# Second attention: the sum of the added columns and the inverse sums at the head of VectorE's step

## The chip, the cores and the metric

The kernel runs on one core of a Trainium2 chip. The metric is the device time of one execution in microseconds (us). A core has five engines with a queue each, which run their instructions in order and meet through semaphores: TensorE (PE, with its weight loads as PEld), VectorE (DVE), ScalarE (ACT), GpSimd (POOL) and SyncE (SP), which issues DMAs.

## The reference

Two blocks of a gated network run over x of 16 batches x 256 rows x 512 columns, each a cross attention and a feed-forward. The part that matters here is the second attention, `_L1_xattn_ref`, with 16 heads of 32 columns:

```python
y_dca, y_main = y[:, -16:, :], y[:, :-16, :]           # 16 added rows, 240 own rows
k_dca = _ln(kv_dca[:, :, 0], kn_dca_w, kn_dca_b);  v_dca = kv_dca[:, :, 1]
q = _ln((x @ Wq + bq).reshape(b, s1, H, HD), qn_w, qn_b)
k = _ln(kv[..., :HD], kn_w, kn_b);  v = kv[..., HD:]
ctx = _attn(q, k, v) + _attn(q, k_dca, v_dca)           # two softmaxes, one sum
return ctx @ Wo + bo
```

Each query row thus has two softmaxes per head, one over 240 columns and one over 16 added ones, each with its own sum.

## The kernel before

The change is in `gated_normed_attention`, the third of four stages of the program (2150 to 2866 us of the span). It runs over 16 batches; a batch has 16 heads in 4 groups of 4, taken in pairs: 8 pairs a batch (`PAIRS`), 128 in all. Every engine has a function `step(i, u)`, called for u from -13 up: `u` is the pair's number (two batches make a turn `i` of the loop), and the order in each queue is the order of the statements in that function. What a batch needs besides its pairs (projections, norms, the output) is placed on steps by a table (`plan`, `due`), with the next batch's work on the steps of the present one. Modulo 8, on VectorE: k0 is taken in step 7 and k1 late in it, q0 in step 1 (late), q1 in 2, v1 in 3, v0 in 4, o0 in 5, o1 in 6; head sums (`head_sums`) are in steps 1 and 3, the statistics in 7, eleven links of an inverse square root (`links`, `root_step`, lines 1903 to 1911) in 3, 4 and 5. A taking reads a projection out of one of two PSUM banks (`room`), adds a bias and frees the bank; TensorE's next product in that bank waits for it (`wait_room`). Batches 2 to 5 (`MADE`) have their k and v loaded from memory: there TensorE has no k and v units, and VectorE's takings of them read SBUF.

A pair n goes this way. TensorE makes the scores (line 2066). VectorE, in step n-1, takes the negated maxima (2530, 2531) and adds that of the 16 added columns (2533). ScalarE, in step n, takes the exponential of the added columns (2180, `d_done`) and of the own ones in four pieces, whose sums it accumulates (2182, an activation and an accumulator read each; `e_done` after the last). In even steps the last two pieces stand behind the copies `copy_pt` and `ot_hi`, which wait for TensorE. VectorE, in step n+1, sums the added columns' exponentials (2491, `d_summed`) and takes the inverse of both sums (2504, `r_done`), which waits for `e_done` and `d_summed`. GpSimd multiplies the probabilities with it (2275 the added columns, 2277 twice the own ones, `p_done`), and then has in some steps the scaling of a group of q and k (2290), a sum with the output's bias (2300) and the gathers (2260). TensorE, in step n+2, turns both heads (2077) through one bank, `ptb`, which ScalarE copies out each time (2192, `pt_done`), and multiplies with v (2091) once a group is whole. Scaled groups of q and k are turned at line 2055.

Of the kernel before, what the change touches and what calls it, by code (L numbers as in the profile page):

```python
# [9 lines left out]
ALU = mybir.AluOpType  # L10
ACT = mybir.ActivationFunctionType
AX = mybir.AxisListType
# [7 lines left out]
NHEAD1, DCA = 16, 16  # L20
# [1721 lines left out]
def gated_normed_attention(nc, x_in, y_sorted, y_kept, weights, slots, x_out, x_kept, ctx_rows, kv_made, kv_kept, dca_hi, dca_lo, kv_dca, gate, ln_cols, ident, raw_in, raw_out, in_hi, in_lo, rows_next, turned, after, ahead, tag):  # L1742
# [7 lines left out]
    LOOP = 2 * PAIRS  # L1750
# [3 lines left out]
    with ExitStack() as ctx:  # L1754
        def sb(name, shape, dt=F32):
            return ctx.enter_context(nc.sbuf_tensor(tag + name, shape, dt))
# [4 lines left out]
        def sem(name):  # L1761
            used.append(nc.alloc_semaphore(tag + name))
            return used[-1]
# [13 lines left out]
        prob = raw_in[:, 0].rearrange("p u (h t s) -> p u h t s", h=2, t=2)  # L1777
# [8 lines left out]
        rsum, rinv = sb("rsum", [P, 4, 2, 4]), sb("rinv", [P, 4, 2, 4])  # L1786
# [22 lines left out]
        s_ready, s_max, s_bias, d_done, d_summed, e_done, r_done, p_done = (  # L1809
            sem("s_ready"), sem("s_max"), sem("s_bias"), sem("d_done"), sem("d_summed"), sem("e_done"), sem("r_done"), sem("p_done"))  # L1810
# [43 lines left out]
        def live(i, bb):  # L1854
            return not isinstance(i, int) or 0 <= 2 * i + bb < B

        def due(i, u, what):

            found = [(u - x[0], x[1:]) for x in WHEN[what] if (u - x[0]) % PAIRS == 0]
            return [(n // PAIRS,) + x for n, x in found if live(i, n // PAIRS)]  # L1860

        def pair(i, u):

            return not isinstance(i, int) or 0 <= LOOP * i + u < B * PAIRS
# [444 lines left out]
        def _(dve):  # L2309
            V = nc.vector  # L2310
# [60 lines left out]
            def statistics(i, bb):  # L2371
                b = 2 * i + bb
                for t in range(2):
                    l = V.bn_stats(stats[:, t], x2[:, bb % 2, t])
                l.then_inc(stat_done, 1)
# [9 lines left out]
            def head_sums(i, bb, half):  # L2385
                dve.wait_ge(sq_done, 2 * (2 * i + bb) + 2 - half)
                V.tensor_reduce(hsum[:, half * 2 * NHEAD1:(half + 1) * 2 * NHEAD1], sq[:].rearrange("p r (h c) -> p (r h) c", h=NHEAD1),
                                AX.X, ALU.add).then_inc(hsum_done, 1)

            def link(i, bb, k):  # L2390
                b = 2 * i + bb
                if k == 0:
                    dve.wait_ge(hsum_done, 2 * b + 3)
                else:
                    dve.wait_ge(head_done, ROOT * b + k)
                root_step(V, k, head_done, 0, hsum[:], 1.0 / HD, HEAD_EPS, hroot[0][:], hroot[1][:], hrstd[:, bb % 2])

            def first_links():
                for k in range(ROOT):
                    link(0, 0, k)  # L2400

            def links(i, u, at):

                for n, part in [(n, x) for x in range(3) for n in due(i, u - x, "head")]:
                    bb = n[0]
                    k = at - 2 + 6 * part
                    if 0 <= k < ROOT and 2 * i + bb:
                        link(i, bb, k)
# [64 lines left out]
            def step(i, u):  # L2473
# [4 lines left out]
                if u == -5:  # L2478
                    head_sums(0, 0, 0)
                    first_links()  # L2480
                for bb, use in due(i, u - 1, "take"):
                    if use[0] == "v" and 2 * i + bb in MADE:
                        take(i, bb, use)
# [1 line left out]
                    if not (use == "q0" or use == "k0" and 2 * i + bb == 0 or use[0] == "v" and 2 * i + bb in MADE):  # L2485
                        take(i, bb, use)
                links(i, u, 0)
                if pair(i, u - 1):
                    n = u - 1
                    dve.wait_ge(d_done, LOOP * i + n + 1)  # L2490
                    V.tensor_reduce(rsum[:, n % 4, 0], prob[:, n % 4, :, :, 0:DCA].rearrange("p h t s -> p (h t) s"), AX.X, ALU.add).then_inc(d_summed, 1)
                for bb, half in due(i, u, "hsum"):
                    if not (2 * i + bb == 0 and half == 0):
                        head_sums(i, bb, half)
# [3 lines left out]
                    take(0, 0, "k1")  # L2498
                for bb, in due(i, u, "stats"):
                    statistics(i, bb)  # L2500
                if pair(i, u - 1):
                    dve.wait_ge(e_done, LOOP * i + n + 3)
                    dve.wait_ge(d_summed, LOOP * i + n + 1)
                    V.reciprocal(rinv[:, n % 4], rsum[:, n % 4]).then_inc(r_done, 1)
                for bb, in due(i, u, "stats"):
                    aggregate(i, bb)
                for bb, use in due(i, u, "take_late"):
# [17 lines left out]
                if pair(i, u + 1):  # L2525
                    n = u + 1
                    N = LOOP * i + n
                    dve.wait_ge(s_ready, N + 1)
                    s = sc[:, n % 2].rearrange("p h (t s) -> p (h t) s", t=2)
# [22 lines left out]
                if past in (1, 2):  # L2552
                    for c in range(2 * past - 2, 2 * past):
                        turned_low_ahead(c)

            all_steps(dve, step)
    clear(nc, used)

# [643 lines left out]
```

## Time and profile before

| | |
|---|---|
| median of 3 runs | 3543.69 us (3540.34 to 3545.72) |
| the profiled execution, its own time | 3546.12 us |
| its span, first to last instruction | 3544.4 us |
| mean granted TensorE clock | 0.989 |
| busy: PE, PEld, DVE, ACT, POOL | 98%, 85%, 65%, 53%, 38% |

The profile is of one execution. Its busy shares are means over four stages with different limits; the chain that ended last gives 19% to PE's instructions of the final feed-forward and says nothing of this stage, so the stage is read by windows, by waits and by the timelines of its steps. Starts are in us from the span's start. A matmul's end is modelled; the idle time in square brackets is that of the engine just ahead of the row, with what ended it.

### The profile page before, as it was taken

To read this page: it belongs to the slowest core of one execution; us is meant where nothing else is said; L and a number is where in the kernel's file an instruction comes from. 1 tells how busy PE (TensorE), PEld (TensorE's weight loads), DVE (VectorE), ACT (ScalarE), POOL (GpSimd) and SP (SyncE) were. 2 spreads that over 40 slices of the span, in tenths; PEclk is the share of its full clock that TensorE was granted. 3 is DMA by queue.
4 is the path that set the end of the run, shared out by engine and by line. 5 is a ranking of instruction groups with operands and counts; after the bars stand their busy time and mean duration, and the time that the engine had idled before them with its cause. 6 is when DMAs were issued, how large, how long until landed. Compare 5 with 4: busy or idle time off the path is not lost. (4 is left out here: it accounts for less than half of the span.)

```text
span 3544.4 us, 66282 instructions
## 1 busy us (share of the span) xinstructions
PE 3464.4 (98%) x22490; PEld 3000.9 (85%) x22490; DVE 2313.4 (65%) x5703; ACT 1866.7 (53%) x4822; POOL 1339.6 (38%) x1345
## 2 busy tenths in 40 slices
PE   9999999999999999899999998899999989999999
PEld 8999999999999999799999996667777668888887
DVE  6666666656666666576767778787777754545543
ACT  5555555554444444455555554787777743333332
POOL 3222222332333322254544554777777640202020
PEclk9999999999999999899999999999999999999999
DMA  4566666535666665577767764222222245344341
GB/s 166 188 237 236 236 238 237 167 98 189 236 236 233 230 235 167 184 272 251 261 250 261 259 247 143 68 89 67 64 70 64 73 128 160 110 129 126 112 131 48
DMA packets 430862, 611.00 MB, mean 172 GB/s; under 512 B 95120, under 2 KB 226320, under 8 KB 426512
## 3 DMA queue, kind: packets, MB, share of 16 engines
q1 hardware_dynamic: 330128, 394.91, 34.1%
q10 hardware_dynamic: 90208, 179.32, 13.7%
q0 software_dynamic: 10272, 33.63, 2.8%
q8 instruction: 130, 2.13, 0.2%
q14 instruction: 124, 1.02, 0.1%
HBM read 339.34 MB, written 268.44 MB: 171 GB/s over the span
## 5 line engine op out<-in xcount | busy, mean ns | idle before, releaser
L853 POOL TENSOR_TENSOR a_prob<-a_prob,a_rinv 128x512 f32<-128x512 f32 x256 | 266.4, 1041 | 1005.2 <-DVE a_rinv L1071 1005.2
L773 ACT ACTIVATE a_prob<-a_prob,a_low_bias 128x256 f32<-128x256 f32 x512 | 256.5, 502 | 469.7 <-DVE a_low_bias L1062 468.2
L527 PE MATMUL a_pj<-a_xt,in_hi 128*128 128x256 f32 x1024 | 309.8, 302 | 0.1
L1378 POOL TENSOR_TENSOR e_act_hi<-e_act_f,e_zeros 128x256 fp32r<-128x256 f32 x128 | 181.5, 1418 | 308.0 <-DVE e_act_f L1608 308.0
L1392 PE MATMUL e_gb<-e_xt_hi,in_hi 128*128 128x256 f32 x1024 | 291.7, 285 | 1.4 <-DVE e_xt_lo L1587 1.4
L1393 PE MATMUL e_gb<-e_xt_lo,in_hi 128*128 128x256 f32 x1024 | 290.9, 284 | 0.0
L1394 PE MATMUL e_gb<-e_xt_hi,in_lo 128*128 128x256 f32 x1024 | 290.9, 284 | 0.0
L2997 DVE TENSOR_TENSOR raw_in<-turned,raw_in 128x512 f32<-128x512 f32 x224 | 151.9, 690 | 212.5 <-PE turned L2710 209.6
L529 PE MATMUL a_pj<-a_xt,in_lo 128*128 128x256 f32 x1024 | 289.0, 282 | 0.0
L528 PE MATMUL a_pj<-a_xt,in_hi 128*128 128x256 f32 x1024 | 288.8, 282 | 0.0
L901 DVE TENSOR_TENSOR a_ot_lo<-a_avb,a_ot_hi 128x256 fp32r<-128x256 f32 x256 | 108.4, 423 | 258.2 <-ACT a_ot_hi L782 258.0
L2277 POOL TENSOR_TENSOR raw_in<-raw_in,d_rinv 128x480 f32<-128x480 f32 x256 | 254.8, 1015 | 0.0
L1587 DVE TENSOR_TENSOR in_lo<-raw_in,in_hi 128x1024 fp32r<-128x1024 f32 (+1 forms) x160 | 205.6, 1291 | 56.9 <-ACT in_hi L1482 56.3
L2182 ACT ACTIVATE raw_in<-turned,d_nmax 128x240 f32<-128x240 f32 x512 | 232.2, 475 | 0.0
L2192 ACT COPY d_pt<-d_ptb 128x512 f32<-128x512 f32 x256 | 153.7, 600 | 122.4 <-PE d_ptb L2077 122.4
L901 DVE TENSOR_TENSOR a_pt_lo<-a_ptb,a_pt_hi 128x512 fp32r<-128x512 f32 x256 | 175.9, 687 | 56.2 <-ACT a_pt_hi L767 39.4
L527 PE MATMUL a_ob<-in_hi,a_ot_hi 128*128 128x512 f32 x512 | 203.1, 397 | 1.8 <-POOL in_lo L861 1.1
L528 PE MATMUL a_ob<-in_lo,a_ot_hi 128*128 128x512 f32 x512 | 202.7, 396 | 0.0
L529 PE MATMUL a_ob<-in_hi,a_ot_lo 128*128 128x512 f32 x512 | 200.2, 391 | 0.0
L1392 PEld LDWEIGHTS e_gb<-e_xt_hi,in_hi 128*128 128x128 f32 x1024 | 197.7, 193 | 2.7 <-DVE e_xt_lo L1587 1.8
L1393 PEld LDWEIGHTS e_gb<-e_xt_lo,in_hi 128*128 128x128 f32 x1024 | 197.7, 193 | 0.9
L1394 PEld LDWEIGHTS e_gb<-e_xt_hi,in_lo 128*128 128x128 f32 x1024 | 197.7, 193 | 0.0
(478 smaller groups left out, 11299.3 us busy)
## 6 DMA issues: line engine op xcount, KB each, us to landing
raw_in<-in_w_gate SPq DMA_DIRECT2D x39, 2048.0 KB, 8.2
x_sorted<-a_spare ACTq DMA_DIRECT2D x42, 1792.0 KB
y_sorted<-a_spare ACTq DMA_DIRECT2D x42, 1792.0 KB
raw_out<-in_w_out SPq DMA_DIRECT2D x40, 1024.0 KB
in_hi<-w_ops SPq DMA_DIRECT2D x224, 128.0 KB, 2.3
in_lo<-w_ops SPq DMA_DIRECT2D x224, 128.0 KB, 2.4
raw_in<-in_x SPq DMA_DIRECT2D x32, 512.0 KB, 6.1
xt_rows<-a_xt SPq DMA_DIRECT2D x16, 1024.0 KB, 5.9
```

Source lines behind the costliest of these rows:

```text
L527: nc.tensor.matmul(out, a_hi, b_hi, start=start, stop=False)
L528: nc.tensor.matmul(out, a_hi, b_lo, start=False, stop=False)
L529: return nc.tensor.matmul(out, a_lo, b_hi, start=False, stop=stop)
L773: e = nc.scalar.activation(prob[:, u % 4, t], prob[:, u % 4, t], ACT.Exp, bias=low_bias[:, u % 2, t:t + 1], scale=-1.0, accum_out=rsum[:, ...
L853: nc.gpsimd.tensor_tensor(prob[:, u % 4], prob[:, u % 4], rinv[:, u % 2].unsqueeze(2).to_broadcast([P, 2, S]), ALU.mult).then_inc(p_done, 1)
L901: return nc.vector.tensor_tensor(out, raw_in, hi.bitcast(F32), ALU.subtract)
L1392: nc.tensor.matmul(out, a_hi, b_hi, start=start, stop=False)
L1393: nc.tensor.matmul(out, a_hi, b_lo, start=False, stop=False)
L1394: return nc.tensor.matmul(out, a_lo, b_hi, start=False, stop=stop)
L1587: return nc.vector.tensor_tensor(out, raw, hi.bitcast(F32), ALU.subtract)
L2182: e = nc.scalar.activation(p[:, j, t, DCA:], s[:, j, t * S + DCA:(t + 1) * S], ACT.Exp, bias=nmax[:, n % 2, 1, 2 * j + t:2 * j + t + 1], a ...
L2277: T(p[:, j, :, DCA:], p[:, j, :, DCA:], r[:, 1, 2 * j:2 * j + 2].unsqueeze(2).to_broadcast([P, 2, S - DCA]), ALU.mult).then_inc(p_done, 1)
```

## The change

The two instructions of a pair on VectorE, the sum of the added columns and the inverse of the sums, with the waits on `d_done`, `e_done` and `d_summed`, are moved from two places further down in VectorE's step to its head, one right behind the other. They pass the takings, the links with `at` 0 to 2, the head sums and the statistics. Nothing else is edited.

```diff
--- before.py
+++ after.py
@@ -2478,6 +2478,13 @@
                 if u == -5:
                     head_sums(0, 0, 0)
                     first_links()
+                if pair(i, u - 1):
+                    n = u - 1
+                    dve.wait_ge(d_done, LOOP * i + n + 1)
+                    V.tensor_reduce(rsum[:, n % 4, 0], prob[:, n % 4, :, :, 0:DCA].rearrange("p h t s -> p (h t) s"), AX.X, ALU.add).then_inc(d_summed, 1)
+                    dve.wait_ge(e_done, LOOP * i + n + 3)
+                    dve.wait_ge(d_summed, LOOP * i + n + 1)
+                    V.reciprocal(rinv[:, n % 4], rsum[:, n % 4]).then_inc(r_done, 1)
                 for bb, use in due(i, u - 1, "take"):
                     if use[0] == "v" and 2 * i + bb in MADE:
                         take(i, bb, use)
@@ -2485,10 +2492,6 @@
                     if not (use == "q0" or use == "k0" and 2 * i + bb == 0 or use[0] == "v" and 2 * i + bb in MADE):
                         take(i, bb, use)
                 links(i, u, 0)
-                if pair(i, u - 1):
-                    n = u - 1
-                    dve.wait_ge(d_done, LOOP * i + n + 1)
-                    V.tensor_reduce(rsum[:, n % 4, 0], prob[:, n % 4, :, :, 0:DCA].rearrange("p h t s -> p (h t) s"), AX.X, ALU.add).then_inc(d_summed, 1)
                 for bb, half in due(i, u, "hsum"):
                     if not (2 * i + bb == 0 and half == 0):
                         head_sums(i, bb, half)
@@ -2498,10 +2501,6 @@
                     take(0, 0, "k1")
                 for bb, in due(i, u, "stats"):
                     statistics(i, bb)
-                if pair(i, u - 1):
-                    dve.wait_ge(e_done, LOOP * i + n + 3)
-                    dve.wait_ge(d_summed, LOOP * i + n + 1)
-                    V.reciprocal(rinv[:, n % 4], rsum[:, n % 4]).then_inc(r_done, 1)
                 for bb, in due(i, u, "stats"):
                     aggregate(i, bb)
                 for bb, use in due(i, u, "take_late"):
```

## Rows read from the trace of the kernel before

**Rows 1.** the four stretches of the pair loop; busy us of each engine, then granted clock, DMA share, GB/s

```profile
2197.00:2250.00 53.00, 46.35 (x282) 32.91 (x283) 36.81 (x87) 39.79 (x131) 35.72 (x43) 0.87 0.20 62
2250.00:2392.00 142.00, 128.59 (x948) 90.47 (x947) 117.59 (x272) 114.97 (x388) 109.87 (x126) 1.00 0.25 82
2392.00:2790.00 398.00, 394.53 (x2758) 286.50 (x2756) 307.09 (x715) 314.80 (x1037) 291.44 (x343) 1.00 0.22 69
2790.00:2866.00 76.00, 67.59 (x445) 44.95 (x444) 45.98 (x118) 52.19 (x169) 38.70 (x50) 0.87 0.12 43
```

**Rows 2.** waits in the ordinary stretch: who waits <- for whom: us, times, longest

```profile
POOL raw_in L2275 <- DVE d_rinv L2504: 93.5, 49, 3.9
...
PE d_pj L1984 <- DVE raw_in L2432: 3.5, 10, 0.3
```

**Rows 3.** timeline of VectorE, ordinary batch, step 7: start us, us, what [idle before <-releaser]

```profile
2516.64 0.69 DVE L2432 TENSOR_TENSOR raw_in<-d_pj,raw_out 128x512 f32<-128x512 f32 x1 [0.56 <-PE d_pj L1986]
...
2518.57 0.18 DVE L2504 RECIPROCAL d_rinv<-d_rsum 128x8 f32<-128x8 f32 x1
```

**Rows 4.** timelines of ScalarE and TensorE, the same step

```profile
2516.28 0.24 ACT L2182 ACTIVATION_READ_ACCUMULATOR raw_in<-turned,d_nmax 128x1 f32 x1
...
2517.38 0.50 PE L1984 MATMUL d_pj<-in_hi,d_ctx 128*128 128x512 f32 x1 [0.35 <-DVE raw_in L2432]
```

**Rows 5.** waits in the loaded stretch

```profile
PE d_ptb L2077 <- ACT d_pt L2192: 10.2, 14, 1.0
...
PE d_ptb L2077 <- POOL raw_in L2277: 2.5, 7, 0.5
```

**Rows 6.** timelines of VectorE, GpSimd, TensorE and ScalarE, loaded batch, steps 5 and 6

```profile
2304.44 0.21 DVE L2491 TENSOR_REDUCE d_rsum<-raw_in 128x4 f32<-128x64 f32 x1
...
2304.75 0.20 DVE L2504 RECIPROCAL d_rinv<-d_rsum 128x8 f32<-128x8 f32 x1
...
2305.03 0.69 POOL L2275 TENSOR_TENSOR raw_in<-raw_in,d_rinv 128x64 f32<-128x64 f32 x1 [3.65 <-DVE d_rinv L2504]
...
2308.67 0.66 PE L2055 MATMUL d_pj<-ident,raw_in 128*128 128x128 f32 x4 [0.16 <-POOL raw_in L2290]
...
2309.37 1.26 ACT L2199 ACTIVATE d_qk<-d_pj,d_ln_sb 128x256 f32<-128x256 f32 x3 [0.25 <-PE d_pj L2055]
```

**Rows 7.** timelines of VectorE and TensorE, first batch, step 1

```profile
2198.86 1.21 DVE L2387 TENSOR_REDUCE d_hsum<-d_sq 128x32 f32<-128x1024 f32 x1
...
2200.49 0.20 DVE L2504 RECIPROCAL d_rinv<-d_rsum 128x8 f32<-128x8 f32 x1 [0.42 <-ACT raw_in L2182]
...
2200.61 0.71 DVE L2424 SCALAR_TENSOR_TENSOR raw_in<-d_pj,d_rstd,raw_out 128x512 f32<-128x512 f32 x1
...
2201.47 0.63 PE L2055 MATMUL d_pj<-ident,raw_in 128*128 128x128 f32 x4
```

**Rows 8.** timelines of VectorE and ScalarE, first batch, step 3

```profile
2207.82 0.69 DVE L2434 TENSOR_TENSOR d_v<-d_pj,raw_out 128x512 f32<-128x512 f32 x1 [0.55 <-PE d_pj L1986]
...
2208.81 0.22 ACT L2182 ACTIVATION_READ_ACCUMULATOR raw_in<-turned,d_nmax 128x1 f32 x1
```

**Rows 9.** timelines of VectorE and GpSimd, ordinary batch, step 4

```profile
2503.18 0.22 DVE L1909 TENSOR_TENSOR d_hroot<-d_hroot 128x64 f32<-128x64 f32 x1
...
2503.85 1.43 POOL L2277 TENSOR_TENSOR raw_in<-raw_in,d_rinv 128x480 f32<-128x480 f32 x1
...
2504.36 1.00 DVE L1907 TENSOR_TENSOR d_hroot<-d_hrstd 128x64 f32<-128x64 f32 x1
```

**Rows 10.** timelines of ScalarE and TensorE, first batch, steps 5 and 6

```profile
2219.21 0.26 ACT L2180 ACTIVATE raw_in<-raw_in 128x64 f32<-128x64 f32 x1 [1.94 <-DVE raw_in L2533]
...
2221.85 1.09 PE L2077 MATMUL d_ptb<-ident,raw_in 128*128 128x128 f32 x4 [2.75 <-POOL raw_in L2277]
```

**Rows 11.** timelines of ScalarE and TensorE, ordinary batch, step 5

```profile
2509.58 0.59 ACT L2192 COPY d_pt<-d_ptb 128x512 f32<-128x512 f32 x1
...
2511.28 0.49 PE L2077 MATMUL d_ptb<-ident,raw_in 128*128 128x128 f32 x3
```

## The prediction

> **What bounds the kernel now.** I read the granted clock first: 0.989 over the span, so the profiled execution is an undisturbed one. Then I cut the stage of the change, the second attention's pair loop, into four stretches [rows 1]: its start (2197 to 2250 us), the batches whose keys and values are loaded instead of computed (2250 to 2392), the ordinary batches (2392 to 2790) and the end. TensorE (PE) is busy 394.53 of 398.00 us in the ordinary stretch, 128.59 of 142.00 in the loaded one, 46.35 of 53.00 in the start, 67.59 of 76.00 in the end. VectorE (DVE) is never above 83%. So PE's queue sets the pace and the change can only take from PE's idle time, or add to it.
>
> Next the waits. In the ordinary stretch GpSimd (POOL) waits 93.5 us for the inverse sums, which is what the change shortens, but PE itself waits only 3.5 us in ten gaps, and for the taking of k0, not for POOL [rows 2]. An earlier inverse sum there feeds an engine that nobody waits for. In the loaded stretch PE waits 10.2 us for ScalarE's (ACT's) copies out of the one transpose bank and 2.5 us for POOL [rows 5].
>
> **The change part by part.** No instruction is added or removed: per pair one 0.21 us reduce and one 0.20 us reciprocal move ahead of takings, head sum, links and statistics, 128 pairs. No DMA is moved and no other queue is edited. What changes is (a) how early the inverse sums come, (b) that DVE's queue now stops at a step's head until ACT has finished the exponentials of the pair before, and everything behind the reciprocal stops with it, (c) which DVE instructions run beside POOL's multiplications. Steps are named by the pair number modulo 8.
>
> *Ordinary batches, step 7.* Here (b) and (a) are both largest. The reciprocal stood at 2518.57, after the statistics; k0's taking started at 2516.64 when PE released it [rows 3]. Pair 6's last accumulator read ends at 2516.28+0.24 = 2516.52, and PE waits for the taking until 2517.38 [rows 4]. So the reciprocal can go at about 2516.56; the next instruction on DVE starts 0.12 later (as 2200.49 to 2200.61 [rows 7]), at about 2516.69: k0's taking is 0.05 us later than now, and PE's gap of 0.35 becomes 0.40. Ten such gaps: +0.5 us. Bounds: 0, if PE's and ACT's order shift together, and the whole reciprocal, 0.20 x 10 = +2.0 us. The reciprocal comes 2.0 us sooner, for nothing.
>
> *Ordinary batches, the other steps.* Steps 1 and 3 also meet exponentials that end just after the head, but their takings wait for PE anyway; at steps 5, 6 and 2 the taking gets some 0.2 to 0.4 us later, and its bank is asked for later than that. Nothing of it reaches PE. What is moved past costs what it cost.
>
> *Step 4 and the port.* The square-root links are 128x64 operations on two SBUF operands. At 2503.18 such a one takes 0.22 us; at 2504.36, with one of POOL's multiplications running (2503.85, 1.43 us), another takes 1.00 [rows 9]: it waits for POOL's instruction to end. Moving the reciprocal forward by some 0.9 us moves POOL's multiplications onto the first links of this step and off the last ones: two links pay about 0.8 us each before and after. One more or one fewer collision is 0.8 us either way; I take 0, plus 0.18 because the reciprocal now stands right behind its sum (2304.44 to 2304.75 is 0.31 us [rows 6], where a filler used to cover all but 0.13). Cover: ACT's copy of pair 3 ends at 2509.58+0.59 = 2510.17 and PE wants it at 2511.28 [rows 11], so up to 1.1 us of lateness is free.
>
> The Trainium skill has this as a rule (page "SBUF — State Buffer", section "SBUF: two separate sides"): VectorE and GpSimd share a port pair as an exclusive lock, taken for a whole instruction, by a VectorE operation with two SBUF inputs against a GpSimd one that reads SBUF. It speaks against the change, since an earlier multiplication meets more such operations in steps 4, 5 and 0. The trace agrees on the lock. Read alone it would have every earlier start paid back by a block; by the row the count of blocks stays two a step, and that is what the sum takes.
>
> *Loaded batches.* In step 5 the reciprocal stands at 2304.75; POOL had idled 3.65 us for it, its scaling of the next group comes behind that, PE's transposes of that group start at 2308.67 after 0.16 us idle for it, and ACT waits 0.25 us for them [rows 6]. Two takings (0.7 us each, as k0's 0.69 [rows 3]) leave the place ahead of the reciprocal; against a somewhat longer step 4 I estimate it 0.8 us sooner, and this chain comes off the path. ACT, on whose copies PE's next three gaps hang, starts 0.25 us sooner. Four batches: -1.0 us. Bounds: 0 (the late links of step 3, whose reciprocal now waits for the exponentials and pushes the head sum back, could eat it) and -3.1 us, all that PE waits for POOL in this stretch: 2.5 us at the probabilities [rows 5] and 4 x 0.16 at the group's transposes [rows 6]. The 10.2 us for ACT's copies stay: ACT works through them back to back.
>
> *Start of the stage.* Here nothing covers (b). At step 1 of the first batch the reciprocal is held until 2200.49 by pair 0's exponentials, while the head sum (1.21 us, from 2198.86) filled that wait; the q0 taking followed at 2200.61, and PE's transposes into the same bank started at 2201.47 without a gap [rows 7]. After the change the head sum comes behind the reciprocal, q0's taking some 1.13 us later, and PE stands for 1.1 us. At step 3 v1's taking ran at 2207.82, but pair 2's last accumulator read ends at 2208.81+0.22 = 2209.03 [rows 8]: taking and head sum move back 1.25 us, less 0.12 for the reciprocal no longer behind it, less 0.2 that DVE waited for PE at the end of that step: +0.9. This reaches PE, as ACT waits 1.94 us for DVE at 2219.21 and PE 2.75 us at 2221.85, behind step 4 [rows 10]; that step adds its 0.2. Sum +2.2 us. Bounds: 0 and, with TensorE's clock, more: the start has a mean granted clock of 0.87 over 53 us [rows 1], about 14 us at the lower of its two levels (1.2 GHz), and the fall is at the 2.75 us gap: the four transposes behind it take 1.09 us [rows 10] where those at 2308.67 take 0.66 [rows 6]. A longer gap may lengthen that; a quarter more would cost 14/4 at half speed, 1.7 us, twice that 3.4 us.
>
> *End of the stage.* The last batch has no takings of keys or queries, so both moved instructions already stand at the head. 0. Its clock (0.87 over 76 us, about 20 us at the lower level [rows 1]) isn't touched.
>
> **Sum.** +0.5 - 1.0 + 2.2 = +1.7 us on the profiled execution's 3546.12 us, 3547.8. That execution is 2.43 us above the median of the runs, so the median should be 3545.4 us.
>
> **Rivals.** (1) *The relief reaches PE.* If the waits that PE spends on POOL go in both stretches where it has them (3.1 in the loaded one [rows 5, 6], the 2.75 of the start [rows 10]) and the clock then falls later or not at all in the start (14 us at half speed, 7 us), the time is 3543.7-5.9 = 3537.8, with the clock 3530.8. For it: POOL idles 93.5 us for exactly this value. Against: at each of those PE gaps the last to come is ACT's copy, or DVE's maximum, not the multiplication. (2) *The lock makes it slower.* The place is step 4, in each of the 15 batches that have one with links. If three links rather than two collide, and the weighted addition too, step 4 grows by more than the 1.1 us of cover [rows 11], and what is above it comes every batch; with 0.8 us above, 15 x 0.8 = 12 us: 3545.4+12 = 3557.4. It decides from two added collisions on. For it: rows 9 show 0.8 us apiece. Against: POOL has just two long instructions to collide with, and DVE in return loses its collision in step 3. (3) *It does nothing:* step 1 and 3 of the start are caught by slack that I don't see, or what is gained and lost cancels: 3543.7.
>
> **How the numbers follow.** My forecast 0.66, rival 1 0.07 (half of it with the clock, below 3536.6), rival 2 0.12, rival 3 0.15. A measurement of this kernel can tell 0.2%, 7.1 us. Faster by more than that needs the clock: 0.05. Slower by more: rival 2 nearly whole, and the forecast's high end with a longer low clock: 0.13. Within: 0.82. The range: down to the forecast's lower bounds (copied and start relief in part), 3539; up to steady +2.0, start +2.2 and clock +3.4, 3543.7+7.6 = 3551.
>
> **What would show it.** Right: in step 7 the reciprocal some 2 us before the statistics' end, k0's PE gaps near 0.40, still ten, and POOL's wait for the inverse sums much below 93.5 with PE's busy time in the ordinary stretch unchanged; in the start a new PE gap of about 1 us at the transposes of line 2055. Wrong: more or less time between two of those gaps than now, gaps at line 2077 in the ordinary stretch, or a start that isn't later.

## The result and the profile of the changed kernel

The changed kernel takes 3553.83 us (median of 7 runs, 3552.16 to 3555.94) against 3540.82 (7 runs) of the kernel before: ratio 1.0033, 95% interval 1.0022 to 1.0045. It is 13.0 us slower. The forecast was 3545.4 with a range up to 3551. The profiled execution took 3552.16 us, with a span of 3550.4 us at a granted clock of 0.993. Of the experiments' executions one, of recip_fwd, took 9811.65 us, against 3550.92 to 3552.19 of its nine others; it is in none of the ratios.

In the lines of the changed kernel the sum stands at L2484, the reciprocal at L2487 and the maximum at L2529 and L2530 (before: L2491, L2504, L2530 and L2531). First the four stretches again, columns as in [rows 1].

```profile
2197.00:2250.00 53.00, 44.73 (x300) 30.65 (x298) 36.25 (x86) 40.41 (x138) 37.14 (x44) 0.94 0.18 57
2250.00:2392.00 142.00, 123.63 (x902) 87.51 (x900) 119.40 (x264) 110.46 (x372) 103.63 (x121) 1.00 0.26 82
2392.00:2790.00 398.00, 388.66 (x2723) 281.98 (x2722) 313.67 (x703) 310.93 (x1023) 282.63 (x340) 1.00 0.23 69
2790.00:2866.00 76.00, 67.63 (x477) 46.49 (x477) 50.99 (x130) 57.87 (x191) 42.17 (x54) 0.93 0.12 43
```

PE's busy time in the ordinary stretch falls from 394.53 to 388.66 us of the same 398, where the forecast had it unchanged, and in the loaded stretch from 128.59 to 123.63. DVE's busy time rises by 6.58 us in the ordinary stretch, with no instruction added. (The windows are the same microseconds and not the same work: in the changed kernel a little less work falls into each.) What PE waits for there, from the view of waits (who <- for whom: us, times, longest):

```profile
POOL raw_in L2275 <- DVE d_rinv L2487: 85.1, 37, 3.8
...
PE d_pj L2055 <- DVE d_x_sb L2437: 5.9, 9, 0.7
...
PE d_pj L1984 <- DVE raw_in L2432: 3.5, 10, 0.3
```

The ten waits for k0's taking are as in [rows 2]. New in the ordinary stretch are nine waits of 0.65 us: PE's transposes of a group's queries and keys (L2055) write a bank that DVE frees in step 6 with the taking of o1, the output block added to the tokens (L2437). In the loaded batches the same wait is 1.51 us, in place of the 0.16 us for POOL [rows 6]. Timelines of PE in the changed kernel, one gap of each kind (start us, us, what, idle before):

```profile
2201.06 0.63 PE L2055 MATMUL d_pj<-ident,raw_in 128*128 128x128 f32 x4 [0.93 <-DVE raw_in L2424]
...
2267.80 0.63 PE L2055 MATMUL d_pj<-ident,raw_in 128*128 128x128 f32 x4 [1.52 <-DVE d_x_sb L2437]
...
2517.88 0.63 PE L2055 MATMUL d_pj<-ident,raw_in 128*128 128x128 f32 x4 [0.66 <-DVE d_x_sb L2437]
```

A measure that leaves out phases is the time from one gap to the same gap a batch later; in the loaded and ordinary stretches, where the granted clock is 1.00, it leaves out the clock too. Ordinary: 42.20 us against 41.55 before, +0.65, nine batches. Loaded: 41.16 against 39.80, +1.36, four batches. The first batch (from PE's gap of 0.72 us near 2196 to the gap of 0.58 near 2250) takes 53.85 us, against 51.7 in executions of the old order with the same clock there (below), +2.2. 5.9+5.4+2.2 = 13.5 us, against 13.0 measured.

Where the 0.65 comes from is seen on DVE and POOL in steps 5 and 6. Timelines of the kernel before (rows that the prediction had not read): reciprocal, weighted addition of an expert's output (L2366), maximum, and the o1 taking, then POOL, and PE with its scores of pair 6 and the transposes.

```profile
2508.56 0.21 DVE L1911 SCALAR_TENSOR_TENSOR d_hrstd<-d_hroot,d_hrstd 128x64 f32<-128x64 f32 x1
...
2509.00 0.20 DVE L2504 RECIPROCAL d_rinv<-d_rsum 128x8 f32<-128x8 f32 x1
2509.12 0.70 DVE L2366 SCALAR_TENSOR_TENSOR d_x<-rows_next,weights,d_x 128x512 f32<-128x512 f32 x1
2509.90 0.23 DVE L2530 TENSOR_REDUCE d_nmax<-turned 128x4 f32<-128x64 f32 x1
...
2511.49 0.75 DVE L2437 SCALAR_TENSOR_TENSOR d_x_sb<-d_pj,d_gate_t,d_x_sb 128x512 f32<-128x512 f32 x1 [0.16 <-PE d_pj L1986]
...
2509.28 0.69 POOL L2275 TENSOR_TENSOR raw_in<-raw_in,d_rinv 128x64 f32<-128x64 f32 x1 [3.05 <-DVE d_rinv L2504]
...
2508.72 1.13 PE L2066 MATMUL turned<-d_qk 32*128 32x256 f32 x8
...
2512.92 0.66 PE L2055 MATMUL d_pj<-ident,raw_in 128*128 128x128 f32 x4
```

And the same places in the changed kernel:

```profile
2512.31 0.20 DVE L2487 RECIPROCAL d_rinv<-d_rsum 128x8 f32<-128x8 f32 x1
2512.43 0.74 DVE L2437 SCALAR_TENSOR_TENSOR d_x_sb<-d_pj,d_gate_t,d_x_sb 128x512 f32<-128x512 f32 x1
2513.09 0.82 DVE L1911 SCALAR_TENSOR_TENSOR d_hrstd<-d_hroot,d_hrstd 128x64 f32<-128x64 f32 x1
2513.83 1.49 DVE L2366 SCALAR_TENSOR_TENSOR d_x<-rows_next,weights,d_x 128x512 f32<-128x512 f32 x1
2515.24 0.21 DVE L2529 TENSOR_REDUCE d_nmax<-turned 128x4 f32<-128x64 f32 x1
...
2517.00 0.73 DVE L2437 SCALAR_TENSOR_TENSOR d_x_sb<-d_pj,d_gate_t,d_x_sb 128x512 f32<-128x512 f32 x1
...
2512.59 0.29 POOL L2275 TENSOR_TENSOR raw_in<-raw_in,d_rinv 128x64 f32<-128x64 f32 x1 [3.83 <-DVE d_rinv L2487]
2512.84 1.93 POOL L2277 TENSOR_TENSOR raw_in<-raw_in,d_rinv 128x480 f32<-128x480 f32 x2
2514.73 1.49 POOL L2290 TENSOR_TENSOR raw_in<-raw_in,d_hrstd 128x512 f32<-128x512 f32 x1
...
2513.00 1.13 PE L2066 MATMUL turned<-d_qk 32*128 32x256 f32 x8
```

Before, the weighted addition stood right behind the reciprocal: it started 0.12 us after it, ahead of POOL (0.28 us after it), took 0.70 us, and POOL's short multiplication paid (0.69 instead of 0.29 us). Now the o0 taking stands between. POOL gets going first, and the link (0.82 instead of 0.21) and the addition (1.49 instead of 0.70) pay: +1.4 us in one step. Not every DVE instruction pays: in these two steps the ones with two operands in SBUF grow, while maximum, sum, reciprocal and the takings out of a bank keep their times beside the same multiplications. (Step 3 has an exception with one operand; see only34.) The addition doesn't wait for all that POOL has queued: it gets in behind the second multiplication, and POOL's scaling (L2290), which comes next, takes 1.49 us where it took 1.04 before.

Set against PE's own position (its scores of pair 6 start at 2508.72 before and at 2513.00 after), the maximum is 1.06 us later than before (2509.90-2508.72 = 1.18, 2515.24-2513.00 = 2.24) and the o1 taking 1.23 us later (2.77, 4.00). Before, the taking ended at 2511.49+0.75 = 2512.24 and PE's transposes went at 2512.92, without a gap, 0.68 us later. In the changed kernel they go 0.15 us behind the taking's end (2517.73, 2517.88), so the slack was below 0.6 us. 1.23 less that is the gap.

In a loaded batch DVE is late by more. Step 5 and the o1 taking there, before and then changed:

```profile
2305.49 0.22 DVE L2530 TENSOR_REDUCE d_nmax<-turned 128x4 f32<-128x64 f32 x1
...
2307.05 0.75 DVE L2437 SCALAR_TENSOR_TENSOR d_x_sb<-d_pj,d_gate_t,d_x_sb 128x512 f32<-128x512 f32 x1
```

```profile
2304.91 1.49 DVE L2366 SCALAR_TENSOR_TENSOR d_x<-rows_next,weights,d_x 128x512 f32<-128x512 f32 x1
2306.32 0.21 DVE L2529 TENSOR_REDUCE d_nmax<-turned 128x4 f32<-128x64 f32 x1
...
2308.08 0.73 DVE L2437 SCALAR_TENSOR_TENSOR d_x_sb<-d_pj,d_gate_t,d_x_sb 128x512 f32<-128x512 f32 x1
```

Against the same scores of PE (2304.30 and 2303.23) the maximum of step 4 is 0.8 us late (2301.39, 2301.08), that of step 5 1.9 us and the taking 2.1 us. So steps 3 and 4 hand on 0.8 us, step 5 adds 1.1, and 2.1 less the slack is the gap of 1.51.

### The profile page after: what moved, and what is told of

Same layout as the page of the kernel before. It is cut to its first block and busy times, and to the rows that moved or that the text cites. A ratio compares the mean times of both kernels' runs of the same rounds, so it can differ in the third digit from the quotient of the medians.

```text
span 3550.4 us, 66282 instructions
## 1 busy us (share of the span) xinstructions
PE 3453.3 (97%) x22490; PEld 2992.1 (84%) x22490; DVE 2330.7 (66%) x5703; ACT 1869.5 (53%) x4822; POOL 1331.1 (37%) x1345
## 3 DMA queue, kind: packets, MB, share of 16 engines
q14 instruction: 124, 1.02, 0.1%
```

## The experiments

All on the change's own place in DVE's step. "New order" is the block of sum and reciprocal at the head, "old order" the two at their old places. The table gives, from each trace, the first batch, the mean loaded and ordinary batch (us from gap to gap), PE's gaps in a loaded batch at the group's transposes and at the turned block (L1984), its gap at the transposes in an ordinary batch, and the time against the kernel before, timed on the same chip. There were three chips, on which the kernel before took 3542.56 us (not5 to recip_fwd), 3539.43 (control to rest) and 3541.74 (addfirst to only34), so kernels of different groups are compared by ratio, and a time just outside an expected range says little by itself. Of addfirst the trace lacks the first row of the first batch. Before's first batch ran more at TensorE's lower level (see *The clock* below).

| kernel | first | loaded | gaps loaded | ordinary | gap ordinary | ratio, 95% interval |
|---|---|---|---|---|---|---|
| before | 54.75 | 39.80 | 0.16, none | 41.55 | none | |
| changed | 53.85 | 41.16 | 1.51, none | 42.20 | 0.65 | 1.0033 [1.0022, 1.0045] |
| not5 | 53.83 | 41.35 | 0.92, 0.73 | 41.49 | none | 1.0010 [1.0000, 1.0019] |
| not6 | 54.06 | 42.23 | 1.09, 1.47 | 41.76 | 0.23 | 1.0027 [1.0017, 1.0036] |
| noport | 53.87 | 40.31 | 0.67, none | 41.49 | none | 1.0004 [0.9994, 1.0013] |
| recip_fwd | 53.50 | 41.56 | 0.86, 1.01 | 42.01 | 0.45 | 1.0023 [1.0013, 1.0033] |
| control | 51.67 | 39.58 | none | 41.49 | none | 0.9995 [0.9985, 1.0004] |
| only5 | 51.75 | 39.99 | 0.35, none | 41.95 | 0.41 | 1.0015 [1.0005, 1.0024] |
| not57 | 53.93 | 40.84 | 0.91 and 1.34, none | 41.49 | none | 1.0019 [1.0010, 1.0029] |
| rest | 51.64 | 40.85 | 0.92 and 1.33, none | 41.49 | none | 1.0009 [0.9999, 1.0019] |
| addfirst | - | 40.38 | 0.75, none | 41.52 | none but one of 0.25 | 1.0010 [1.0001, 1.0020] |
| not357 | 51.49 | 40.09 | 0.41, none | 41.74 | 0.17 | 1.0009 [1.0000, 1.0019] |
| only7 | 52.17 | 40.58 | 0.16, 0.72 | 41.55 | none | 1.0004 [0.9994, 1.0013] |
| only34 | 52.83 | 41.04 | 0.88 and 1.27, none | 41.49 | none | 1.0017 [1.0008, 1.0027] |

**not5.** The new order in all steps but 5. Its edit, and with other conditions that of not6, only5, not57, rest, not357, only7 and only34:

```diff
-                if pair(i, u - 1):
+                if pair(i, u - 1) and (u % 8 != 5):
                     n = u - 1
```

with the two old places under the opposite condition.

> The change in all steps except step 5 (pair number modulo 8), which keeps the old order: taking of o0, link, sum, reciprocal, weighted addition. Port theory: the time is lost in step 5, where POOL's multiplications now start before the link (line 1911) and the weighted addition (line 2366) and block them (0.82 us instead of 0.21, 1.49 instead of 0.70); with step 5 as before, the gap of TensorE at line 2055 behind o1's taking (0.66 us in ordinary batches, 1.51 in loaded ones) is gone or under 0.1 us in the ordinary ones and near the old 0.16 in the loaded ones, and the time is 3540 to 3544 us. Order theory: what delays o1's taking is that sum and reciprocal stand ahead of it in step 6 (0.43 us), whatever step 5 does; then the 0.66 us gaps stay and the time is near the changed kernel's 3553.8 us.

3547.29 us, above what was expected. The ordinary batches went as forecast: the gap at L2055 is gone and the batch takes 41.49 us. The rest was missed: the loaded batches didn't recover, they wait 0.92 us for POOL at the transposes and 0.73 us at a new place. So without step 5 there is no ordinary loss, and the loaded one has further sources.

**not6.** The new order in all steps but 6.

> The change in all steps except step 6, where o1's taking stands ahead of sum and reciprocal again. Port theory: VectorE still enters step 6 about 1.1 us late out of step 5, o1's taking is late by that less the 0.26 us it had waited for TensorE or lain behind, against 0.57 us of slack: a gap of 0.2 to 0.3 us at line 2055 in ordinary batches, about 1.1 in loaded ones, time 3546 to 3549 us. Order theory: the gaps are gone, 3540 to 3543 us.

The ordinary gap is 0.23 us, inside what was expected: of the 1.23 us of lateness 0.43 is sum and reciprocal ahead of the taking itself (2516.57 to 2517.00 in the changed kernel), and taking only those away leaves the collisions. The time, 3552.81, was missed, and again through the loaded batches: 1.47 us at the turned block, from one DVE instruction that took 3.38 us. It is k1's taking (L2432), which in a loaded batch adds a bias to rows in SBUF; the expectations call it the centring.

```profile
2275.11 3.38 DVE L2432 TENSOR_TENSOR raw_in<-raw_in,raw_out 128x512 f32<-128x512 f32 x1
...
2281.55 0.47 PE L1984 MATMUL d_pj<-in_hi,d_xt_hi 128*128 128x512 f32 x1 [1.47 <-DVE d_xt_lo L2312]
```

**noport.** The changed kernel with step 5's weighted addition replaced by a reduce over the same 128x512 block, which has one operand. Part of the sum over the experts is left out.

```diff
+                if k == 0 and t == 1:
+                    V.tensor_reduce(scrap[:], y_sb[:, t, k].rearrange("p (h c) -> p h c", h=NHEAD1), AX.X, ALU.add).then_inc(sum_done, 1)
+                else:
+                    V.scalar_tensor_tensor(x2[:, bb % 2, t], y_sb[:, t, k], ... [the line as it was]
```

> The changed kernel with the weighted addition of step 5 (the third of a batch's four, slot 0 of the second half of the rows) left out; a reduce over the same 128x512 elements of the gathered rows stands in its place, one SBUF operand instead of two and about the same length (0.67 us). Port theory: the reduce does not wait for POOL's multiplication, the link at line 1911 still does (0.6 us too long): VectorE is 0.3 to 0.6 us late out of step 5 instead of 1.1, the gap at line 2055 is 0 to 0.2 us in ordinary batches, time 3541 to 3546 us. Order theory: the order of the queue is unchanged, the gap stays 0.66 us, 3553 us.

3543.92 us: the loss of the ordinary batches is gone (41.49 us, no gap at the transposes). Timeline of DVE, then of POOL; the replacement takes 0.67 us right beside POOL's multiplications, and the link ahead of it still pays:

```profile
2509.55 0.82 DVE L1912 SCALAR_TENSOR_TENSOR d_hrstd<-d_hroot,d_hrstd 128x64 f32<-128x64 f32 x1
2510.29 0.67 DVE L2368 TENSOR_REDUCE d_scrap<-rows_next 128x16 f32<-128x512 f32 x1
2510.89 0.21 DVE L2541 TENSOR_REDUCE d_nmax<-turned 128x4 f32<-128x64 f32 x1
...
2509.30 1.93 POOL L2278 TENSOR_TENSOR raw_in<-raw_in,d_rinv 128x480 f32<-128x480 f32 x2
```

The new order of the queue is the same here, wait included. So the order with its stop at the reciprocal costs the ordinary batches nothing by itself: the o1 taking is then some 0.4 us late (3.17 us behind PE's scores, 2.77 before), inside the slack. The 0.8 us that the addition waits for POOL take it out. Once they do, the order's 0.43 us count too: not6, without them, has a gap of 0.23 in place of 0.65.

**recip_fwd.** Sum and reciprocal stay behind takings and first links, where the sum stood; the reciprocal alone moves forward, past head sum, links and statistics.

> The block of sum and reciprocal stands where the sum stood before: behind the takings and the first link, ahead of head sums, further links and statistics. Only the reciprocal moves. Port theory and order theory alike: step 5 and step 6 are what they were, no gap at line 2055, time 3540 to 3543 us, and the reciprocal of step 7 is still over 1 us earlier. If instead the wait for the exponentials ahead of head sums is what costs (a third theory, of the queue blocked at the wait), the time is above 3547 us.

3551.37: missed by both theories as I had put them, and above the 3547 of the third, the queue blocked at the wait. Nothing stands ahead of the takings here, and the loss is nearly that of the change. The trace doesn't bear the third theory out in ordinary batches: in steps 3 to 5 the reciprocal goes 0.31 us behind the sum, with no idle time for the exponentials, and noport and addfirst have that wait in every step and lose nothing there. Steps 3 and 4 of an ordinary batch show what does it, DVE and then POOL:

```profile
2504.73 0.91 DVE L1905 TENSOR_SCALAR d_hrstd<-d_hroot 128x64 int32<-128x64 int32 x1
...
2508.99 0.20 DVE L2501 RECIPROCAL d_rinv<-d_rsum 128x8 f32<-128x8 f32 x1
...
2509.68 0.91 DVE L1911 SCALAR_TENSOR_TENSOR d_hrstd<-d_hroot,d_hrstd 128x64 f32<-128x64 f32 x1
2510.52 1.49 DVE L2366 SCALAR_TENSOR_TENSOR d_x<-rows_next,weights,d_x 128x512 f32<-128x512 f32 x1
...
2509.53 1.93 POOL L2277 TENSOR_TENSOR raw_in<-raw_in,d_rinv 128x480 f32<-128x480 f32 x2
```

In step 3 the integer link pays (0.91 us, 0.20 before), in step 4 the addition (1.49, 0.85 before); step 5's addition doesn't (it stands right behind the reciprocal and takes 0.70). DVE enters step 4 0.25 us late against PE's scores and step 5 0.46 us; step 5's inverse sum is 0.47 us late with it, and PE waits 0.45 us, now for POOL's operand of the transposes. The same mechanism, one and two steps earlier. So such a loss comes without anything ahead of the takings, and my expectation had been too narrow: I had looked for collisions only in step 5.

**control.** The kernel before with the reduce of noport (the same part of the sum left out).

> The kernel before, with the same weighted addition (the one of step 5) replaced by a reduce of equal length as in noport, so that noport has a partner in the old order. Part of the sum over the experts is left out. In the old order this addition takes 0.70 us beside no multiplication, so nothing should change. Port theory: no gap at the group's transposes in the ordinary stretch, period 41.54 us, loaded period 39.8 us, 3541 to 3544 us. If the replaced addition were by itself worth something (less traffic, less work), this kernel would be faster than the one before by as much as noport is faster than the changed one, 8 to 10 us: 3532 to 3535.

3537.95 us, 3 us below the port theory's range, but on this chip the kernel before took 3539.43 us: the ratio is 0.9995, the same as before, which is what that theory said. Its interval leaves the replacement at most 5 us (0.15%) of its own; the ordinary batch is 41.49 us with it and 41.55 without, which is 0.5 us in all, and the loaded ones give 0.9 us. Of the 0.71 us per ordinary batch that it brings in the changed kernel all but this 0.06 is the collision's.

**only5.** The new order in step 5 alone.

> The new order in step 5 alone, the old one in the other seven. Theory A: step 5 alone holds the two collisions that count, so its gap is that of not6 (0.23 us), as not6 and this kernel both keep the old order in step 6: 0.2 to 0.3 us at the group's transposes in nine ordinary batches, period 41.8 us; in the loaded ones 0.5 to 1.1 us more than the 0.16 of before; start not later than before. 3545 to 3549 us. Theory B: the lateness is gathered over steps 3 to 6 and step 5 by itself stays inside its cover: no gap in ordinary batches, 3541 to 3544.

3544.65 us. Step 5 by itself makes 0.40 us a batch (41.95 against 41.55), more than expected but of the right kind; nothing has to gather over earlier steps. The first batch is not later, as forecast.

**not57, only7.** These two ask where the second new gap of the loaded batches comes from.

> The new order in all steps but 5 and 7. In not5 the second centring of step 7 of a loaded batch took 2.79 us (0.76 before) beside two of GpSimd's instructions in a row, and PE then stood 0.73 us for the low half of the turned block. Theory A (that block comes from the early multiplication of step 7): with the old order in step 7 the 2.79 and the gap of 0.73 are gone, four batches, 2.9 us: 3544 to 3545 us; loaded period 40.6; the gap of 0.9 at the group's transposes stays. Theory B (the step is late from before, steps 3 to 6): the gap stays, 3547 as not5. Ordinary period 41.5 us by both.

> The new order in step 7 alone. Ordinary batches: the prediction had k0's gap go from 0.35 to 0.40, the changed kernel shows 0.35; here too 0.35 and a period of 41.5 us. Loaded batches: if the second centring of step 7 is starved (2.79 us in not5) by an early multiplication of its own step, it is so here, with a gap of up to 0.7 us for the low half of the turned block, period 40.0 to 40.6; if it takes the lateness of the steps before too, neither shows: 39.8. 3540 to 3543 us.

only7 has it by itself. DVE and POOL in step 7 of a loaded batch, and PE:

```profile
2266.86 0.66 DVE L2432 TENSOR_TENSOR raw_in<-raw_in,raw_out 128x512 f32<-128x512 f32 x1
...
2268.98 2.78 DVE L2432 TENSOR_TENSOR raw_in<-raw_in,raw_out 128x512 f32<-128x512 f32 x1
...
2268.05 1.93 POOL L2277 TENSOR_TENSOR raw_in<-raw_in,d_rinv 128x480 f32<-128x480 f32 x2
2269.94 1.26 POOL L2300 TENSOR_TENSOR d_x_sb<-d_x,raw_out 128x512 f32<-128x512 f32 x1
...
2274.82 0.47 PE L1984 MATMUL d_pj<-in_hi,d_xt_hi 128*128 128x512 f32 x1 [0.71 <-DVE d_xt_lo L2312]
```

The taking of k1, due at 2268.98, stays behind the second of POOL's two multiplications and the whole of the next operation: they follow each other without a break and DVE doesn't get in between. It ends only at 2271.76. In not57 the gap of 0.73 us is gone, as the first theory had it, but its time isn't: ratio 1.0019, no better than not5's 1.0010. In the traces more than half of it comes back at the transposes (three gaps of 0.73 us go, and three of 0.92 become 1.34); the rest lies inside the intervals. I hadn't foreseen that. only7 is within what can be told from the kernel before. Its ordinary batches show k0's gap unchanged at 0.35.

**rest.** As not57, the first batch in the old order too.

> As not57, and the first batch wholly in the old order: the new order stands in steps 0 to 4 and 6 of the second batch and after. Start theory: the new gap of 0.93 us at the first transposes (the q0 taking behind the reciprocal) goes, and the long gap at the probabilities goes back from 3.23 to 2.75 us: 1.4 us less than not57, unless TensorE then spends longer at its lower clock, as before the change (0.87 against 0.94 mean in the first 53 us), which would give back up to 3.5 us. 3542 to 3547 us. If earlier inverse sums are worth something anywhere, this kernel, without the three places that lose, is the one to show it: below 3541.

The first batch is back at 51.64 us, and 3543.71 us is 3.7 less than not57. In the traces the wait at step 1 and the later v1 taking cost 2.3 us, about what the prediction said. There is nothing below 3541: the earlier inverse sums are worth nothing that shows (in ordinary batches 41.49 against 41.55 us, 0.5 us in all).

**only34.** The new order in steps 3 and 4 alone, the place of the prediction's second rival.

> The new order in steps 3 and 4 alone, in all batches. This is the place of the prediction's second rival (three or more collisions in step 4, beyond its cover of 1.1 us). That rival: ordinary period 42 us or more, 3548 and above. Port theory as the changed kernel shows it: step 4 keeps two collisions in ordinary batches, no gap, 41.5 us; in the loaded ones the multiplications on the operand of the group's transposes come late by 0.7 to 1.1 us and PE stands 0.9 to 1.3 us for them, 3 to 4.5 us in all; at the start v1's taking moves back 1.25 us, some 0.5 us of PE's time. 3543 to 3546 us.

Its ordinary batches are untouched (41.49 us): in step 4 two links collide before and two after (the changed kernel shows 0.61 and 0.91 us), as the prediction's sum had it. The second rival's 42 us and more didn't come; the time, 3547.09 us, is 1 us above the range of the port theory. The loaded ones lose 1.2 us each: the gap at the transposes is 0.88 and 1.27 us, in turn. In step 3 there the integer link, with one operand in SBUF, takes 0.91 us beside POOL:

```profile
2249.59 1.93 POOL L2277 TENSOR_TENSOR raw_in<-raw_in,d_rinv 128x480 f32<-128x480 f32 x2
...
2250.66 0.91 DVE L1905 TENSOR_SCALAR d_hrstd<-d_hroot 128x64 int32<-128x64 int32 x1
```

**not357.** As rest, step 3 in the old order too.

> As rest, with the old order in step 3 too: the new order stands in steps 0, 1, 2, 4 and 6 from the second batch on. In rest the loaded batches lose some 1.1 us each at the group's transposes (0.92 and 1.36 against 0.16). In step 3 of a loaded batch the new order let the integer link beside GpSimd's multiplication take 0.91 us (0.20 before), and the step ended 0.35 us later. Theory A (steps 3 and 4 share the lateness): the gap goes back by 0.3 to 0.5 us, to 0.5 to 0.9: 3541 to 3543 us. Theory B (step 3 alone): back to 0.16 and 3540. Theory C (step 4 alone): the gap stays near 0.9 to 1.3.

The loaded gap falls from 0.92 and 1.33 to 0.41 us: about three quarters are step 3's, somewhat more than the first theory gave it. The time, 3544.39 us, is above every theory's. In exchange the ordinary batches get a gap of 0.17 us for POOL's operand, which no theory had: another arrangement of collisions.

**addfirst.** The changed kernel with step 5's weighted addition ahead of sum and reciprocal. The whole work is done.

```diff
+                for bb, k, t in due(i, u, "sum") if u % 8 == 5 else []:
+                    add_expert(i, bb, k, t)
```

At the addition's old place the loop has `if u % 8 != 5 else []`, so each addition is done once.

> The changed kernel, and in step 5 the weighted addition goes ahead of the sum and the reciprocal, so that it runs while GpSimd still waits for the inverse sums. All work is done, nothing is left out. Port theory: the addition takes 0.7 us instead of 1.49, the link behind the taking collides as before; what comes behind step 5 is 0.7 to 0.8 us sooner than in the changed kernel, the taking of o1 0.45 us late against a slack of 0.57: no gap at the group's transposes in the ordinary batches, period 41.5 us; in the loaded ones 0.7 us instead of 1.51. 3544 to 3547 us. If the taking is late because the queue stops at the reciprocal, or the lock only goes over to another operation, the gap of 0.65 stays: 3552 to 3555 us.

As the port theory had it: 3545.03 us, no gap at the transposes in the ordinary batches but one (0.25), 0.75 us instead of 1.51 in the loaded ones. The addition runs while POOL waits:

```profile
2510.68 0.74 DVE L2366 SCALAR_TENSOR_TENSOR d_x<-rows_next,weights,d_x 128x512 f32<-128x512 f32 x1
...
2511.65 0.20 DVE L2489 RECIPROCAL d_rinv<-d_rsum 128x8 f32<-128x8 f32 x1
...
2512.42 0.83 DVE L1911 SCALAR_TENSOR_TENSOR d_hrstd<-d_hroot,d_hrstd 128x64 f32<-128x64 f32 x1
```

One instruction moved by a few places gives back most of the loss (1.0010 in place of 1.0033). It still isn't faster than the kernel before (1.0001 to 1.0020), nor is any other of these kernels that does the whole work.

**What stays open.** How much of a loaded batch's loss is due to which step doesn't add up from the single kernels: only5, only7 and only34 give 0.2, 0.8 and 1.2 us, the changed kernel 1.36 in all, since a step that enters late misses one collision and meets another. And the sum over the batches of a trace agrees with the timed difference only to some 4 us, about what the intervals leave.

## Why the prediction was wrong

Of the sum's terms the one for the other steps of ordinary batches stood at nothing and measured +5.9 us, the one for the loaded batches stood at -1.0 and measured +5.4; step 7 (+0.5) measured nothing and the start (+2.2) came.

*The bound.* Right: PE's queue set the pace, and nearly all that the change did came as PE gaps (the start has 0.7 us of another kind, below).

*Step 7, ordinary.* The place and mechanism were right, the +0.05 us didn't come: k0's taking goes 0.16 us after the last accumulator read instead of 0.12, but takes 0.65 instead of 0.69 us, and the gap stays 0.35. The reciprocal is 2.0 us ahead of the statistics' end, as predicted.

*The other steps, ordinary.* This is the step that failed: "at steps 5, 6 and 2 the taking gets some 0.2 to 0.4 us later, and its bank is asked for later than that. Nothing of it reaches PE." The own part was sized well (0.43 us in step 6). Three things were missed. The slack of the o1 taking, below 0.6 us, wasn't worked out. Step 5 was never searched for collisions, though it holds a 128x512 operation on two SBUF operands. And it wasn't asked which of the two engines gets in first: the old order let the addition start 0.16 us ahead of POOL, the new one lets POOL in. +1.4 us there, +0.65 at PE, nine times; noport and addfirst, which take away this collision by two different means, bring the batch back to 41.49 and 41.52 us.

*Step 4.* Right in its place: two collisions before and after, and nothing reaches PE in ordinary batches (only34). The mistake was to carry "the count of blocks stays two a step" over to steps that I hadn't counted. The second rival had the mechanism, the sign and nearly the size (12 us, 3557.4), but the wrong step; at 0.12 it was given too little for a price of 0.8 us that can fall on any of DVE's operations with two SBUF operands.

The Trainium skill (page "SBUF — State Buffer", section "SBUF: two separate sides") says that whichever of the two engines starts first has the port pair for its whole instruction. The pairs 0.70 with 0.69 us before and 1.49 with 0.29 us after are this rule at work; I had cited it and used it for a count alone. It names operations of DVE with two SBUF inputs, or in its two-port modes. The 0.91 us of the integer link, which has one input, is outside the first of these; no run here shows which mode it was in.

*Loaded batches.* Wrong in sign: -1.0 forecast, +5.4 measured. The reciprocal does come earlier in step 5 (by 0.6 us against PE's scores, 0.8 forecast) and POOL's scaling ends 0.2 us sooner, as the forecast's chain wanted. But the instructions behind it in DVE's queue are late, by 0.8 us out of steps 3 and 4 and 1.1 more in step 5, and the group's transposes wait for the o1 taking instead. No PE gap for ACT's copies shrank: these stay at 0.58, 1.02 and 0.28 us. How the loss divides between the steps stays open, as said.

*Start.* Right: a new gap of 0.93 us at L2055 (forecast 1.1), the gap at the probabilities from 2.75 to 3.23 us, and about 2.2 us in all (rest, not57), as summed. That the sum fits so well is in part luck: PE's idle time grows by only 1.5 us against control (6.2 to 7.7), less than the 2.2 of the terms. The other 0.7 is longer busy time of PE (44.9 to 45.6 us over the first batch), which no run explains.

*End.* As forecast, nothing of the change: PE's gaps stand at the same distances until the clock falls. From the last k0 gap to the end the profiled execution of before took 3.2 us more, with PE busy 89.3 us for the same work in place of 84.8 (granted clock 0.89 against 0.95).

*The clock.* The terms for TensorE's lower level don't hold. Mean granted clock in the first 53 us was 0.87 before and 0.94 after, but control has 0.94 too, with the same gap of 2.75 us, and addfirst 0.86. It differs between executions, and no run ties it to the order. It also explains why the profiled execution of before lay above its median: its first batch took 54.75 us against 51.7 in control and rest, with PE busy 47.8 us for the same work in place of 44.9, and the end took those 3.2 us.

*Rival 1* needed relief at the waits for POOL. POOL's wait for the inverse sums in the ordinary stretch went down by only 9% (93.5 to 85.1 us), and no PE wait went with it. POOL's idle time didn't even shrink: in the changed kernel it waits 15.7 us for a DMA (0.2 before), at L2300. The prediction's argument against this rival, that the multiplication is nowhere last, isn't what its rows say, since [rows 5] and [rows 10] name POOL. It held all the same: the loaded gaps of 0.48 and 0.27 us that the profile had put to POOL are as long after the change, and are put to ACT's copy.

## What to carry to other kernels

Before an instruction that releases GpSimd is moved, look at what VectorE runs in the 0.3 us behind it: an operation on two SBUF operands right behind the release got in first here (0.12 us against 0.28), and one placed behind another instruction waited for GpSimd's running multiplication, sometimes for the next operation too. Do this for every step that has such an operation, not for the one that looks fullest, and write the slack of each taking beside it. An engine's idle time (93.5 us of it here) is no reason to feed it earlier when nobody waits for what it makes.

## What the runs showed of the hardware

A VectorE operation on two SBUF operands doesn't always get in between two GpSimd operations that follow each other: k1's taking took 2.78 us in only7 and 3.38 in not6, against 0.66 us for k0's. In the changed kernel's step 5 the addition did get in, and GpSimd's scaling behind it took 1.49 us instead of 1.04. What decides between the two no run shows. The other way round GpSimd pays in the same way (its multiplication of 128x64 took 0.69 instead of 0.29 us). A reduce of 128x512 ran in 0.67 us beside the same multiplications that held the addition for 1.49. And a 128x64 integer link with one SBUF operand was held as well, 0.91 us instead of 0.20, and the f32 link ahead of it (L1903) took 0.60 in the changed kernel instead of 0.20.
